# A decoder layer on one core: cross attention weighs its values two groups at a time

## The reference, cut to what matters

```python
q1, q2 = (q[..., :sd], q[..., sd:])
k1, k2 = (k[..., :sd], k[..., sd:])
a1 = jax.nn.softmax(jnp.einsum('bhtd,bhsd->bhts', q1, k1) * SCALING, axis=-1)
a2 = jax.nn.softmax(jnp.einsum('bhtd,bhsd->bhts', q2, k2) * SCALING, axis=-1)
diff_weights = a1 - lam * a2
attn_output = jnp.einsum('bhts,bhsd->bhtd', diff_weights, v)
attn_output = attn_output * (1.0 - LAMBDA_INIT)
output = attn_output @ out_proj_weight.T + out_proj_bias
```

## Time and profile before

| | |
|---|---|
| median of 3 runs | 1929.56 us (1927.08 to 1930.03) |
| the profiled execution's own time | 1931.76 us |
| its span in the profile | 1930.1 us |
| busy in the span | PE 1605.4 us (83%), DVE 1148.1 (59%), ACT 908.6 (47%), POOL 745.2 (39%) |
| granted clock of PE over the whole span | 0.928 |
| `cross`, from its first maxima to its last step | 481.6 to about 1167 us |

### The profile page before, as it was taken

How to read it: one execution, slowest core, us unless ns; L and a number is a source line. 1 busy time by engine, 2 the same in 40 slices (tenths; PEclk the granted TensorE clock), 3 DMA queues, 4 the chain that set the end, 5 groups by cost and what they waited for, 6 DMA issues and landing times. The chain is left out here.

```text
span 1930.1 us, 46415 instructions
## 1 busy us (share of the span) xinstructions
PE 1605.4 (83%) x17662; PEld 1215.9 (63%) x17662; DVE 1148.1 (59%) x2505; ACT 908.6 (47%) x2160; POOL 745.2 (39%) x928
## 2 busy tenths in 40 slices
PE   4899999982999999999999980009999999999960
PEld 2666666661566666666666650008888888888860
DVE  4566666652888888888888854004444444444434
ACT  1344444451576676676666760004444444444422
POOL 5333333322256656656656662730111111111116
PEclk9999999995899999999999995559999999999985
DMA  6666666623355555555555525345666666666627
GB/s 167 180 183 181 177 177 183 176 84 64 102 145 140 150 148 139 151 147 139 153 146 140 152 92 138 118 154 194 229 230 230 230 230 230 230 230 230 230 103 284
DMA packets 213973, 328.35 MB, mean 170 GB/s; under 512 B 68888, under 2 KB 179128, under 8 KB 213752
## 3 DMA queue, kind: packets, MB, share of 16 engines
q1 hardware_dynamic: 198104, 258.41, 44.6%
q0 software_dynamic: 15648, 66.97, 9.6%
HBM read 233.30 MB, written 91.67 MB: 168 GB/s over the span
## 5 line engine op out<-in xcount | busy, mean ns | idle before, releaser
L958 DVE TENSOR_REDUCE cross_mx<-cross_bank_max 112x2 f32<-112x750 f32 x512 | 464.6, 933 | 99.2 <-PE cross_bank_max L1001 93.9
L890 ACT ACTIVATE cross_probs<-cross_bank_score 125x448 f32<-125x448 f32 x768 | 407.6, 541 | 203.8 <-PE cross_bank_score L991 200.7
L1490 PE MATMUL experts_bank_h<-experts_x_hi,experts_w 128*128 128x256 f16 x2240 | 372.1, 273 | 7.0 <-DMA experts_w<-w_halves 7.0
L1490 PE MATMUL experts_bank_h<-experts_x_lo,experts_w 128*128 128x256 f16 x1120 | 306.1, 273 | 0.0
L1448 DVE TENSOR_TENSOR experts_hid<-experts_bank_h,experts_gated 128x256 f32<-128x256 f32 x280 | 118.5, 423 | 290.3 <-ACT experts_gated L1387 290.2
L991 PE MATMUL cross_bank_score<-cross_qst,cross_kst 97*125 97x448 f16 x768 | 285.6, 373 | 1.9 <-issue 1.1
L1001 PE MATMUL cross_bank_max<-cross_kst,cross_qst 96*112 96x375 f16 x1024 | 254.7, 331 | 29.4 <-DMA cross_val<-cross_v 27.8
L1361 POOL DMA_INDIRECT y<-experts_y,experts_dest_i x70 | 67.1, 959 | 516.6 <-ACT experts_y L1399 506.0
L1490 PEld LDWEIGHTS experts_bank_h<-experts_x_hi,experts_w 128*128 128x128 f16 x2240 | 219.5, 98 | 33.0 <-issue 7.4
L824 POOL TENSOR_SCALAR cross_ew_big<-cross_ew 128x512 f32<-128x512 f32 x96 | 143.4, 1494 | 173.9 <-DMA cross_ew<-in_experts 173.9
L1015 PE MATMUL cross_bank_out<-cross_probs,cross_val 125*32 125x112 f32 x6144 | 200.5, 263 | 0.1
(11 more groups left out here) (224 smaller groups left out, 2718.4 us busy)
## 6 DMA issues: line engine op xcount, KB each, us to landing
experts_w<-w_halves SPq DMA_DIRECT2D x35, 3072.0 KB, 11.5
cross_ew<-in_experts POOLq DMA_DIRECT2D x32, 768.0 KB, 6.1
w_halves<-cross_ew_half POOLq DMA_DIRECT2D x32, 768.0 KB, 6.6
cross_kst<-cross_k SPq DMA_DIRECT2D x96, 187.5 KB
cross_v<-front_v SPq DMA_DIRECT2D x24, 531.2 KB
cross_val<-cross_v SPq DMA_DIRECT2D x32, 398.4 KB
front_src<-in_ctx_t SPq DMA_DIRECT2D x24, 500.0 KB, 8.5
experts_rows<-routed SPq DMA_DIRECT2D x35, 260.0 KB, 6.1
```

Source lines behind the costliest of these rows:

```text
L890: nc.scalar.activation(probs[:, e % PROBS], bank_score[e % 2][0:SC, 0:4 * T], ACT.Exp, scale=CROSS_SCALE).then_inc(probs_ready, 1)
L958: nc.vector.tensor_reduce(mx[:, b % nb, 2 * n:2 * n + 2], bank_max[n % 2][0:T, :, 0:S], AX.X, ALU.max).then_inc(max_read, 1)
L1490: last = nc.tensor.matmul(bank_h[f % 4][:, mat * BLOCK:(mat + 1) * BLOCK], w13(p, wh, mat, k, f), xt[:, p, k], start=n == 0, stop=n == len ...
```

## The change

`PROBS` goes from 6 to 12: twelve tiles of probabilities in SBUF instead of six. The weighing is no longer issued at k = 1 of every group for the group before, but at k = 1 of every even group for the two groups before it, one right behind the other. The maxima (two units per instruction), the steps, the places of the copies and all other instructions stay as they are. Within an item, bursts stood at e = 1, 4, 7, 10, 13, 16, 19, 22 with one group each; they stand at e = 1 (groups 6 and 7 of the item before), 7, 13 and 19 with two groups each.

```diff
-PROBS = 6
+PROBS = 12
 UNITS = 2 * H
 GROUPS, CHUNKS = UNITS // 4, S // SC
...
                         if k != 1 and on(c + lead):
                             maxima(c + lead, 2 * g + k // 2)
-                        if k == 1:
-                            b, before = (c, g - 1) if g else (c - 1, GROUPS - 1)
+                        if k == 1 and g % 2 == 0:
+                            b, before = (c, g - 2) if g else (c - 1, GROUPS - 2)
                             if on(b):
                                 weigh(b, before)
+                                weigh(b, before + 1)
```

## The result

The changed kernel took 1942.33 us in the median of 11 runs (1936.37 to 1949.67), the kernel before 1933.38 beside it (1927.08 to 1942.18). The ratio is 1.0044, 95% interval 1.0023 to 1.0064: a little slower, by more than a measurement needs. The prediction said no change, 1929.5 us, range 1920 to 1941.

A forecast was written before the change was run, and what follows sets the result against it. PE was taken to set the pace, with DVE 2.9 us an item to spare. Terms of -1.1 - 0.53 - 0.47 + 2.1 = 0.0 us an item left the time unchanged, 1929.5 us against the median, range 1920 to 1941.

The forecast's parts named there:

- four borders of a burst: On PE, a group costs less inside another burst than alone: 0.27 us saved a merger, 1.1 us an item.
- `heads`: This PE step's wait for DVE's normalising gets covered by the longer burst at e = 7: 0.53 us saved an item.
- `turn`: This PE step's wait for the normalising of e = 18 gets covered: 0.47 us saved an item.
- stalls at e = 5, 11, 17, 23: Scores with no burst between wait for ACT's exponential two before: 0.71, 0.10, 0.57 and 0.31 us more an item.
- stall at `proj`: PE's `proj` waits for ACT's copy of `heads_t`, which the burst of e = 10 covered: 0.43 us more an item.
- The chain at e = 5: ACT's copy of `bank_out` and `neg_mx` delay exponential 3, so score 5 starts at 2.09 against 1.38: 0.71 us stall.
- D: Rival: a group costs the same in a burst as alone, so the 1.1 us fall away: +35 us, 1965; chance 0.03.
- C: Rival: DVE becomes the bound as merged bursts hold back maxima pairs: +16 us, 1946; chance 0.08.
- B: Rival: the stalls behind ACT add up with their late ends, 0.25 us an item: slower, 1937.5; chance 0.12.
- At nothing: List of effects put at no cost: more probability tiles, the copies, SP's loads, the last item's bursts.
- the side that had 0.23: The chance given to the changed kernel being slower, beside 0.27 for faster and 0.50 for same.
- Against the median: The profiled execution, 1931.8 us, was taken as 2.2 over the median, so the forecast was put at 1929.5 us.

The follow-up runs named there:

- 13: Kernel before with only the values and `x_in` sent ahead of `row1`: 1918.25 us, ratio 0.9916 to before.
- 14: Changed kernel with only the values and `x_in` sent ahead of `row1`: 1918.50 us, ratio 0.9927 to before.
- 15: As 14, with ACT's copies of `bank_out` one chunk later, at e = 15 and e = 3: 1901.64 us, ratio 0.9839 to before.
- 1: Kernel before with `PROBS = 12` and the bursts left as they were: 1935.89 us, ratio 0.9989 to before.
- 4: Kernel before with the next item's negated maxima made at e = 16 instead of 15 on ACT: 1936.74 us, ratio 1.0002 to before.
- 8: Changed kernel with only the next item's negated maxima made at e = 14 instead of 15 on ACT: 1946.79 us, ratio 1.0048 to before.
- 5: Changed kernel with the values and `x_in` sent behind the row for e = 0 instead of ahead: 1923.13 us, ratio 0.9929 to before.
- 6: Kernel before with the values and `x_in` sent behind the row for e = 0: 1932.04 us, ratio 0.9984 to before.
- 2: Changed kernel with ACT's copies of `bank_out` at e = 15 and 3 instead of 14 and 2: 1932.54 us, ratio 0.9976 to before.
- 10: Changed kernel with all three ACT places moved, values and `x_in` ahead of `row1`, and POOL loading the next item's experts' weights earlier: 2061.99 us.

## Why the prediction was wrong, step by step

The pair 13 and 14 lets each term be read as the mean distance between two scores. The table is in us an item, 14 minus 13; "stalls" is what a distance in 14 has over the same one without a wait (0.20 between two plain scores).

| term | forecast | measured |
|---|---|---|
| four borders of a burst | -1.1 | 4 x (0.57 - 0.80) = -0.92, and -0.06 for score 5, which waited a little in 13 |
| `heads` | -0.53 | 0.74 - 1.30 = -0.56 |
| `turn` | -0.47 | 0.76 - 1.28 = -0.52 |
| stalls at e = 5, 11, 17, 23 | +0.71, +0.10, +0.57, +0.31 | +0.65, +0.06, +0.54, +0.27 |
| stall at `proj` | +0.43 | 1.99 - 1.45 = +0.54 |
| sum | 0.0 | 0.0 |

- **The savings and the stalls were right**, within 0.18 each, and so was their balance. The merger saves 0.23 and not 0.27: behind a burst as behind a wait a score has 0.24 us to its maxima, so at e = 5 the 0.04 that I counted as saved stays, and the 0.05 from the end of an exponential to the score that waits is half of what I took. The chain at e = 5 is settled by 15 as well: with the copy out of it the distance falls from 0.85 to 0.47.
- **D did not happen.** The second group of a burst costs 0.57 us, as read from the starts within a burst. The Trainium skill, "TensorE: Matmul & The Clock Gate", in the section on packing small matmuls, lets a load overlap only with matmuls of other row groups; here loads of 125 rows stay hidden inside a burst (24 starts in 0.57 us, each matmul lasting 0.26), and the measurement decides. **C did not happen** either: PE's loads wait 15.9 us in all for DVE's reductions after and 9.8 before, and DVE is no busier. **B** came near in time (1937.5) by another cause: the stalls did not add up late, they came out 0.06 below the forecast.
- **The step that failed** is in the part "At nothing": "SP's loads wait for the burst at e = 1, which stays." The burst stays, but it takes 1.29 us instead of 0.71, and `row1` stands behind it. So the row for e = 12 is sent 3.68 us into an item instead of 3.10 and, since SP issues in this order, the load behind it 0.58 later as well (4.29 for 3.71). The row for e = 0 is sent later too, at 14.9 instead of 14.2. In the median the last piece of the load lands 18.8 us into an item instead of 17.8 (over the 20 items for which both traces have it), the row for e = 0 at 19.7 instead of 18.7. The item is no longer than before, so from that landing to the next item's first score 0.8 us is left of 1.7, and where the load is slow the row is late. The prediction put all this at nothing: it followed what the longer burst holds back on PE, ACT and DVE and took SP's queue at a sentence, with no landing read.
- **What it came to.** The late waits are 6.8 us in after and 1.5 before, +5.3. The two bursts at the lower clock add 2.7. Together 8.0 of the 10.3 us by which the stretch from item 0's first score to item 31's is longer (648.3 against 638.0 us); most of the rest lies in the distances just behind the falls of the clock (0.48, 0.58 and 0.36 us more in item 27). The median is 9 us longer. That is a comparison of two executions (1931.76 and 1939.54 us), each somewhat faster than its kernel's median. Three traces have the bursts where before has them (before, 1, 4): late waits of 1.5, 4.0 and 4.4 us, stretches of 638.0, 641.0 and 644.4. Two have them where after has them, with ACT's copies in place (after, 8): 6.8 and 7.3 us, 648.3 and 650.0. By their means the change adds 3.8 us of late waits, not 5.3, and 8 us in all. The price of a late row was also not foreseen in kind: in after, 2 us of wait cost 3.5 with the clock.
- **How far this is shown.** Experiments 5 and 14 take the two large transfers from ahead of the row and leave everything else of the change; the late waits and the slow bursts go in both, and between 13 and 14 nothing is left of the 9 us. Experiment 8 rules out that the row's place against the weights' load decides, and that sending the row 0.44 us sooner is enough. Each of these edits moves other transfers in time as well, and no run made the row alone late by a full microsecond in before (4 sent it 0.36 us later, and the median stayed). So far it is shown that late rows make the change slower. Open is the size of the shift: the row's landing moved by 1.0 us, the start of the load by 0.58, and the issue of its last piece hardly (10.36 us into an item before, 10.42 after, in the median). SP's issuing of the twelve pieces of `qst` does not make it: it takes 4.19 us in the median of both, though 5.5 in the two items of after with the long waits. POOL's store of the split weights (L831, 768 KB) is sent at 10.9 and 11.0 us, beside the values, and lands at 17.8 and 18.2; what it does to the load was not tried.
- **The numbers.** 1942.33 lies 1.3 us over the range's upper end, and on the side that had 0.23. "Against the median" cost some too: the kernel before took 1933.4 to 1936.7 us beside the experiments, not 1929.56, which was the median of three runs. So part of the absolute miss is the base; the ratio, 0.44% instead of none, is the miss of the mechanism.

## What to carry to other kernels

When a change makes one engine's wait longer, look in every DMA queue for what is sent behind it, and read the landing of the first small transfer that a loop's next turn needs: here a row of 3.5 KB behind a slow load arrived 0.2 us after the load's last piece. Here merging bursts of one engine traded their borders and two waits for stalls behind its neighbours, and what that comes to depends on the waits that stood there (nothing in 13 and 14, 8.9 us in 5 and 6). It pays once the neighbour's work is moved out of the gaps (here one chunk of ACT each, -0.9% and -0.7%). Then the critical row, the large load and the other engines' loads each need a stretch of their own: with all of it the same kernel is 2.3% faster than the one before (1893.17 us).

## What the runs showed of the hardware

- **A small transfer waits for the queue.** A row of one size took 1.7 us to land alone, 7.7 behind a load in the same queue, and 9.8 beside two loads. In before and after the row for e = 0 never lands ahead of the last piece of the load ahead of it, in the items that could be read: it lands 0.2 to 2.4 us behind, and 0.2 in the items with the longest waits.
- **A wait can cost nearly twice, but its length does not tell.** After 2.0 us without a matmul PE went from 1.00 to 0.50 and the next burst took 1.1 us more; waits of 0.99 us and less, in before and after, did not do that. Elsewhere late waits of 1.05 us (2) and 1.10 (8) were followed by 0.50 at the next burst, and 2.00 (4), 1.65 and 2.16 (8) were not.
- **Moving a load in time can cost 6%.** The same 768 KB of weights, sent beside the values instead of later, made PE wait for another transfer by up to 5.2 us an item. The one execution of 10 at 1900.14 us did not pay it.
- **VectorE held by GpSimd.** The small product L936 takes 0.17 us at its shortest and up to 0.88 after (1.11 in the earlier trace rows), and then ends as POOL's L828 does. The Trainium skill, "SBUF — State Buffer", in the section on the two separate sides, describes the port that the two share as an exclusive lock, for a DVE operation with two SBUF inputs against a POOL operation that reads SBUF. The trace agrees. So `heads` depends on where POOL stands in the item: from score 9 to score 10 the mean was 1.30 us in 13, 1.50 in before and 1.70 in 6, with no edit to DVE. L936 took over 0.3 us in 2, 17 and 24 of its 64 instances there. That POOL's place makes the whole of that difference was not tried alone.
